# Attention over 16 heads: some copies of the turned keys moved to VectorE, waits moved to single products, and the next rows' two measures put side by side

## What is computed

```python
qkv = x @ Wqkv.T                                  # x: layernorm(x), b=8, t=512, D=256, 16 heads of 16
q = cos * q + rotate_half(q) * sin
k = cos * k + rotate_half(k) * sin
scores = jnp.einsum('bhqd,bhkd->bhqk', q, k) / math.sqrt(DH)
scores = jnp.where(causal, scores, -jnp.inf)
attn = jax.nn.softmax(scores, axis=-1)
out = jnp.einsum('bhqk,bhkd->bhqd', attn, v)
out = out.transpose(0, 2, 1, 3).reshape(b, t, d) @ Wo.T      # added to x
```

## Time and profile before

| | |
|---|---|
| median of 3 runs | 2533.52 us (2532.68 to 2536.14) |
| the profiled execution, its own time | 2531.52 us |
| its span in the trace | 2529.8 us |
| TensorE busy, share of the span | 2267.8 us, 90% |
| TensorE weight loads | 1748.3 us, 69% |
| VectorE | 1555.9 us, 62% |
| ScalarE | 1315.7 us, 52% |
| GpSimd | 922.6 us, 36% |
| second attention, 604 to 1204 us of the span: TensorE, VectorE, ScalarE, GpSimd busy | 481.69, 373.44, 339.30, 221.12 us |

### The profile page before, as it was taken

How to read it: one execution, slowest core, us unless ns; L and a number is a source line. 1 busy time by engine, 2 the same in 40 slices (tenths; PEclk the granted TensorE clock), 3 DMA queues, 4 the chain that set the end, 5 groups by cost and what they waited for, 6 DMA issues and landing times.

```text
span 2529.8 us, 45343 instructions
## 1 busy us (share of the span) xinstructions
PE 2267.8 (90%) x15874; PEld 1748.3 (69%) x15874; DVE 1555.9 (62%) x4796; ACT 1315.7 (52%) x3214; POOL 922.6 (36%) x1363
## 2 busy tenths in 40 slices
PE   7999599996778788877699999999999999999998
PEld 5777499994445363544567777777777777777777
DVE  6665422224666757565667676777777667776675
ACT  2221133333555755465555675666755675656753
POOL 2221122213434433332543344333544445343451
PEclk9999699998787988878899999999999999999999
DMA  3222411112001010100200000000101000000000
GB/s 132 100 100 90 130 36 37 39 30 79 19 10 59 3 59 11 35 35 11 88 9 18 16 3 18 18 18 10 44 26 62 19 9 26 26 26 18 10 18 26
DMA packets 75937, 96.41 MB, mean 38 GB/s; under 512 B 6113, under 2 KB 69090, under 8 KB 75458
## 3 DMA queue, kind: packets, MB, share of 16 engines
q1 hardware_dynamic: 70786, 81.89, 9.7%
q0 software_dynamic: 3408, 9.31, 1.3%
q10 hardware_dynamic: 1520, 2.31, 0.3%
HBM read 62.69 MB, written 30.28 MB: 37 GB/s over the span
## 4 chain that ended last, share of the span: by engine, by line
PE 27%; DVE 9%; ACT 8%; issue 5%; POOL 3%; DMA 0%; SPq 0%; DVEq 0%; POOLq 0%; ACTq 0%
PE l_free L2194 4%; PE l_free L2196 4%; PE l_free L2195 3%; PE l_out L2309 3%; PE l_score L2269 2%; POOL l_probs L1684 2%; PE l_turned L2290 2%; DVE l_probsT L1779 2%; DVE l_work L1856 2%; PE l_turned L2194 1%; PE l_turned L2196 1%; PE l_turned L2195 1%; DVE l_u_low L1862 1%; ACT l_probs L2068 1%; PE l_turned L2243 1%
## 5 line engine op out<-in xcount | busy, mean ns | idle before, releaser
L1684 POOL TENSOR_SCALAR l_probs<-l_probs,l_rinv 128x256 f32<-128x256 f32 (+1 forms) x512 | 223.5, 456 | 227.6 <-DVE l_rinv L1839 227.5
L1114 DVE CUSTOM_DVE_ANT_0 c_raw<-cbank,c_later 128x256 f32<-128x256 f32 (+3 forms) x512 | 218.3, 487 | 73.3 <-PE cbank L1301 73.0
L2068 ACT ACTIVATE l_probs<-l_probs,l_nmax 128x256 f32<-128x256 f32 (+1 forms) x512 | 239.9, 473 | 26.5 <-DVE l_nmax L1834 26.4
L1217 ACT ACTIVATE c_cprobsT<-cbank 128x384 f32<-128x384 f32 (+1 forms) x384 | 180.9, 525 | 95.8 <-PE cbank L1327 95.7
L1834 DVE CUSTOM_DVE_ANT_0 l_probs<-l_score,mask,l_inv 128x256 f32<-128x256 f32 (+1 forms) x512 | 200.0, 447 | 28.8 <-PE l_score L2269 28.1
L2194 PE MATMUL l_free<-l_part,l_w_high 128*128 128x512 f32 x384 | 166.4, 433 | 9.6 <-DVE l_probsT L1779 6.6
L2194 PE MATMUL l_free<-l_wqkv_high,l_yT 128*128 128x512 f32 x384 | 159.0, 414 | 1.9 <-DVE l_part L1758 1.9
L1817 DVE COPY l_probsT<-l_turned 128x512 f32<-128x512 f32 (+1 forms) x128 | 79.9, 624 | 131.3 <-PE l_turned L2290 80.3
L1006 POOL TENSOR_SCALAR_AFFINE_SELECT c_cprobsT<-c_cprobsT 128x256 f32<-128x256 f32 x256 | 99.6, 413 | 154.3 <-ACT c_cprobsT L1217 152.2
L2196 PE MATMUL l_free<-l_part,l_w_low 128*128 128x512 f32 x384 | 153.0, 398 | 0.0
L2195 PE MATMUL l_free<-l_yT,l_w_high 128*128 128x512 f32 x384 | 152.8, 398 | 0.0
(11 more groups left out here) (282 smaller groups left out, 5932.1 us busy)
## 6 DMA issues: line engine op xcount, KB each, us to landing
w<-in_W1T SPq DMA_DIRECT2D x8, 1024.0 KB, 8.0
w<-in_W2T SPq DMA_DIRECT2D x8, 1024.0 KB, 11.8
ys_d<-m_y SPq DMA_DIRECT2D x39, 128.0 KB, 1.7
xn_d<-a_prods SPq DMA_DIRECT2D x8, 512.0 KB, 3.6
c_came<-x_d SPq DMA_DIRECT2D x8, 512.0 KB, 4.9
y_d<-c_raw SPq DMA_DIRECT2D x8, 512.0 KB, 3.7
early_rows<-y_d SPq DMA_DIRECT2D x8, 512.0 KB, 3.7
l_came<-y_d SPq DMA_DIRECT2D x8, 512.0 KB, 3.9
```

The source lines that it names most:

```text
L1114: last = dve.tensor_tensor_reduce(raw[:, CHUNKS - NS + s, h * 2 * P:h * 2 * P + wide], score_place("scores", u, s)[:, h * 2 * P:h * 2 * P ...
L1217: act.activation(probsT[s][:, c % 2, i, k0:k0 + w], turned_place(j, s)[:, 0:w], ACT.Exp).then_inc(probs_ready[s], 1)
L1684: pool.tensor_scalar(a, a, rinv[:, j, r, h:h + 1], 1.0, ALU.mult, ALU.mult).then_inc(normed, 1)
L2068: act.activation(a, a, ACT.Exp, bias=nmax[:, j, r, h:h + 1], scale=-1.0, accum_out=rsum[:, j % 2, r, h:h + 1])\
```

## The change

Six things, all in `phase_attn1`:
- **Keys by VectorE.** For the last three turns of a pair (5, 6, 7) the two halves of the turned keys are copied to kT by VectorE (`keys_out`), after its last `parts`; ScalarE copies only their q. The copies count a semaphore of their own, `late_kT`, and TensorE waits for the one or the other count.
- **Order of the next pair's norm.** For every pair but the first, both rows are measured before the first is scaled.
- **Scores.** Each stream's wait for a free score bank stands at its own first product.
- **Turned scores.** Each stream's wait for exponentials stands at its own first product.
- **Output of the last chunk, part 0,** is made one step later, after piece 46 of the turned scores instead of before it.
- **The waits at unit 0** for all of qT, kT and v stand in a loop of their own.

```diff
--- before.py
+++ after.py
@@ -860,7 +860,7 @@
         qk_psum, v_psum, v_ready = sem2("cqk_psum"), sem2("cv_psum"), sem2("cv_ready")
         turned, rotated, high_ready = sem2("turned"), sem2("rotated"), sem2("high_ready")
         q_split, k_split = sem2("q_split"), sem2("k_split")
-        qkT_psum, qkT_ready = sem2("qkT_psum"), sem2("qkT_ready")
+        qkT_psum, qkT_ready, late_kT = sem2("qkT_psum"), sem2("qkT_ready"), sem2("late_kT")
         scores_ready, nmax_ready, probs_ready = sem2("cscores"), sem2("cnmax_r"), sem2("cprobs_r")
         nmax_high, nmax_split, nmaxT_psum, nmaxT_ready = sem("nmax_high"), sem("nmax_split"), sem("nmaxT_psum"), sem("nmaxT_ready")
         nmax_rows = [sem2(f"nmax_rows{i}") for i in range(2)]
@@ -872,6 +872,14 @@
         turns = [(s, t) for t in range(NT) for s in range(NS)]
         LAG = 3
+        late_keys = turns[-LAG:]
+
+        def copied(s, t, i):
+
+            late = sum(1 for r in range(t + 1) for k in (2, 3) if (s, r) in late_keys and (r, k) <= (t, i))
+            return 4 * t + i + 1 - late, late
+
+        ALL_COPIED = [copied(s, NT - 1, 3) for s in range(NS)]
@@ -1062,8 +1070,12 @@
                         whole_rows(0)
                         row_measure(0)
                         whole_rows(1)
-                        row_norm(0)
-                        row_measure(1)
+                        if trip:
+                            row_measure(1)
+                            row_norm(0)
+                        else:
+                            row_norm(0)
+                            row_measure(1)
                         row_norm(1)
                     def measure(s, done=0):
@@ -1100,6 +1112,12 @@
                         k = cosed[s][:, D:QK].rearrange("p (h d) -> p h d", d=DH1)
                         dve.wait_ge(high_ready[s], pair * (2 * NT) + 2 * (t + 1))
                         dve.tensor_tensor(khl[s][:, :, 3, :], k, khl[s][:, :, 0, :].bitcast(F32), ALU.subtract).then_inc(k_split[s], 1)
+
+                    def keys_out(s, t):
+                        for i in range(2):
+                            dve.wait_ge(qkT_psum[s], pair * (4 * NT) + 4 * t + 3 + i)
+                            dve.tensor_copy(kT[s][:, 4 * i:4 * i + 4, t * P:(t + 1) * P],
+                                            bank[s][2 + i][:].rearrange("p (a b) -> p a b", b=P)).then_inc(late_kT[s], 1)
                     def row_max(s, u):
                         c, qt, i, n = units[u]
@@ -1132,6 +1150,8 @@
                             turn(*turns[i])
                         if i:
                             parts(*turns[i - 1])
+                    for turned_late in late_keys:
+                        keys_out(*turned_late)
                     for u in range(UNITS):
                         for s in range(NS):
                             row_max(s, u)
@@ -1191,7 +1211,7 @@
                     for i in range(len(turns) + LAG):
                         if i >= LAG:
-                            for j in range(4):
+                            for j in range(2 if turns[i - LAG] in late_keys else 4):
                                 qkT_out(*turns[i - LAG], j)
                         if i < len(turns):
                             s, t = turns[i]
@@ -1268,7 +1288,10 @@
                         pe.wait_ge((q_split, k_split)[which][s], pair * NT + t + 1)
                         for i in (2 * which, 2 * which + 1):
                             if 4 * t + i >= 2:
-                                pe.wait_ge(qkT_ready[s], pair * (4 * NT) + 4 * t + i - 1)
+                                by_act, late = copied(s, *divmod(4 * t + i - 2, 4))
+                                pe.wait_ge(qkT_ready[s], pair * ALL_COPIED[s][0] + by_act)
+                                if late:
+                                    pe.wait_ge(late_kT[s], pair * ALL_COPIED[s][1] + late)
                             out = bank[s][2 + i % 2]
                             for a in range(4):
                                 p = 4 * (i % 2) + a
@@ -1288,14 +1311,16 @@
                     def scores(u):
                         c, qt, i0, n = units[u]
-                        for s in range(NS):
-                            if u == 0:
-                                pe.wait_ge(qkT_ready[s], pair * (4 * NT) + 4 * NT)
+                        if u == 0:
+                            for s in range(NS):
+                                pe.wait_ge(qkT_ready[s], (pair + 1) * ALL_COPIED[s][0])
+                                pe.wait_ge(late_kT[s], (pair + 1) * ALL_COPIED[s][1])
                                 pe.wait_ge(v_ready[s], pair * NT + NT)
-                            free_place("scores", u, s)
                         wide = max(2, qt + 1) * P
                         for i in range(n):
                             for s in range(NS):
+                                if i == 0:
+                                    free_place("scores", u, s)
                                 h = head(s, c, i0 + i)
                                 r, p = slice(64 * (h % 2), 64 * (h % 2) + 64), h // 2
                                 last = pe.matmul(score_place("scores", u, s)[:, i * 2 * P:i * 2 * P + wide], qT[s][r, p, qt * P:(qt + 1) * P],
@@ -1312,16 +1337,16 @@
                     def scores_turned(j):
                         c, i, kts = pieces[j]
-                        for s in range(NS):
-                            if j % PER_CHUNK == 0:
+                        if j % PER_CHUNK == 0:
+                            for s in range(NS):
                                 pe.wait_ge(nmax_rows[c % 2][s], pair * (16 * CHUNKS) + 32 * (c // 2 + 1))
-                            m = NS * j + s - 3
-                            if m >= 0:
-                                pe.wait_ge(probs_ready[m % NS], pair * UNITS + m // NS + 1)
                         for kt in kts:
                             q0 = min(kt, NT - 2)
                             at = 2 * P if kt == NT - 1 else 0
                             for s in range(NS):
+                                m = NS * j + s - 3
+                                if kt == kts[0] and m >= 0:
+                                    pe.wait_ge(probs_ready[m % NS], pair * UNITS + m // NS + 1)
                                 h = head(s, c, i)
                                 r, p = slice(64 * (h % 2), 64 * (h % 2) + 64), h // 2
                                 last = pe.matmul(turned_place(j, s)[:, at - (kt - q0) * P:at + (NT - kt) * P], kT[s][r, p, kt * P:(kt + 1) * P],
@@ -1365,7 +1390,11 @@
                         if 0 <= j < UNITS:
                             scores_turned(j)
                         for part in range(3):
-                            if j >= 3 and (j - 3 - 2 * part) % PER_CHUNK == 0 and 0 <= j - 3 - 2 * part < UNITS:
+                            if part == 0 and u == UNITS + SCORE_LAG - 3:
+                                continue
+                            if part == 0 and u == UNITS + SCORE_LAG - 2:
+                                output(CHUNKS - 1, part)
+                            elif j >= 3 and (j - 3 - 2 * part) % PER_CHUNK == 0 and 0 <= j - 3 - 2 * part < UNITS:
                                 output((j - 3 - 2 * part) // PER_CHUNK, part)
                     pe.wait_ge(raw_ready, pair * CHUNKS + CHUNKS)
                     for k in range(2 * NT):
```

## The result

Before: 2533.93 us (2532.68 to 2536.14, 4 runs). After: **2498.40 us** (2497.42 to 2499.67, 4 runs). The ratio is 0.9856 with a 95% interval of 0.9841 to 0.9872, a gain of 35.5 us. I forecast 15.4 us and a range down to 2509 us, so the prediction was wrong: the sign was right, the size less than half. The profiled execution took 2499.67 us.

What follows compares the result with a forecast made beforehand. No engine is full; only waits on the ring of engines count. The terms 1.8 + 6.0 + 2.2 + 1.6 + 3.8 = 15.4 us, taken from 2533.52, gave 2518.1 us (chance 0.63), range 2509 to 2526 us.

Steps and rivals of the forecast that it cites:

- Waits at single products: Turned scores: early stream 0 products save TensorE 2.2 us in whole chunks and 1.6 us in first chunks; bounds nothing and 8.4.
- The tail: End of each pair: piece 46 ahead of part 0 starts piece 47 0.95 us earlier, 3.8 us in four pairs.
- Order of the norm: Tails of pairs 0 to 2: TensorE's waits behind POOL ahead of part 0 go, 6.0 us; bounds nothing and 6.0.
- Part 0 itself: Tail: part 0 of the last chunk's output, now ahead of piece 47, is late next, then the last ban again.
- Bans beside scalings: Tail: POOL's bans beside VectorE's scalings slow by 0.1 us, covered; by the skill's port rule the sum would be 1.1 less.
- Keys: End of the projections: VectorE copying late keys brings the first scores 0.45 us earlier a pair, 1.8 us in four.
- Scores' waits: Scores: loosening stream 0's wait gives nothing, at most 0.3 us a pair, as VectorE works without a gap.
- middle chunks: Sign in the changed profile: a middle chunk of 8.4 instead of 8.53 us; still 8.53 would be wrong.
- only POOL's wait goes: Rival: the small savings, 9.4 us, are taken by whatever ends next; 6 to 8 us less, 2526.5 us; chance 0.16.
- POOL's wait stays: Rival: bans or the power of row set 1 are late for another reason; 2524.1 us; chance 0.07.
- the clock drops in the middle: Rival: split waits for piece 1 lose the upper clock, 1.5 us a middle chunk, 2548 us if all 20; chance 0.04.
- the clock stays up in the tails: Rival: without idleness 2.4 GHz holds in pairs 0 to 2, 2.2 us each, 6.6 more, 2511.5 us; chance 0.10.

Runs made afterwards that it cites:

- turned_alone: The kernel before with only the waits of the turned scores moved to each stream's first product; gain 15.0 us, ratio 0.9936.
- three: The kernel before with the norm's new order, the turned scores' waits at single products and part 0 of the last chunk one step later; 2502.15 us, ratio 0.9889.
- turned_out: The kernel before with the turned scores' waits at single products and part 0 of the last chunk one step later; gain 21.3 us, ratio 0.9923.
- no_norm: The changed kernel with the old order of the next pair's norm; gain 18.9 us against the kernel before, ratio 0.9931.
- fill_begin1: The changed kernel with one extra unread 512-column product in each of a pair's first 11 steps; gain 17.0 us against the kernel before, ratio 0.9936.
- keys_alone: The kernel before with only the late keys copied by VectorE; gain 2.1 us, ratio 0.9994 (0.9984 to 1.0005).
- scores_alone: The kernel before with only the scores' waits at each stream's first product, plus the loop of waits at unit 0; gain 1.5 us, ratio 0.9994.

## Why the prediction was wrong

What bounds the kernel was read rightly: no engine is full, the waits on the ring are what counts, and all but 0.9 of the 31.9 us lie in the four score stages and the joins between them. The medians of the five parts alone sum to 8.9 + 15.0 + 1.5 + 7.9 + 2.1 = 35.4 us, beside a measured gain of 35.5. That is in part luck and doesn't show that the parts simply add: the changed kernel's second measurement gained 31.7, and by the stages of their profiles the five parts come to 13.1 us of the 31.9, and in each of them the clock falls or rises in other places. The steps that failed are sizes.

- **Waits at single products: 3.8 us forecast, 15.0 measured alone** (interval 12 to 21; 9.1 placed by the stages). This step failed most. Two errors are seen in the middle chunk. Piece 1 gave 0.17 us, not 0.11: "saves only the 0.11 us between the two starts" forgot what follows it. (The rows that I named for "not much more than one alone" show no product alone; the line at 829.65 does, 0.39 us against 0.51 for two.) And I took piece 5 at nothing, "ahead of the DMA of the maxima"; it gave 0.10. Together 0.25 us by five chunks by four pairs is 5.0 us, where I had 2.2. The first chunks gave about the rest of the 8.2 us of the middles, 0.8 a pair, where I had 0.4; some of that is the clock, whose rise came 3.6 and 3.0 us after the first output product in pairs 0 and 2 before, and 1.9 and 1.8 after. And the tail, where I counted no wait of this kind for itself, gave 2.6 us more in joins and last tail. My upper bound of 0.3 us for each of 28 waits, 8.4 us, is what the middles gave (8.2, or 6.5 in turned_alone); I had it in the text and chose less than half of it.
- **The tail: 3.8 forecast, 7.2 in the stages, 7.9 by the median.** Piece 46 ahead of part 0 gave 1.5 us in pairs 0 and 1 alone and 1.3 in pair 3, where I took 0.95: about the whole step of 1.46 us from piece 46 to 47, which I had as upper bound. In pairs 0 to 2 part of it is POOL's delay, hidden behind piece 46, which I had given to the norm alone. "Part 0 itself" was late next, as predicted, and moving it again brought piece 47 only 0.45 us forward and no shorter tail.
- **Order of the norm: 6.0 forecast, 7.3 and 8.9 measured alone.** The mechanism is as told: powers side by side at 862.40, bans at 864.42, no wait for POOL ahead of part 0. The sum of idle times was a fair price alone, and too low in company: 7.7 us (three against turned_out) or 16.6 (the changed kernel against no_norm), both from medians on two chips. The step took the arrival of TensorE at part 0 from the trace of before, and other parts move it: the wait came to 8.7 us with the single waits alone, and back to 6.0 with the step later beside them (no_norm). "Bounds: nothing and 6.0" failed even alone. Pair 0's tail became 4.2 us shorter with a wait of 2.73, because the clock, counted separately as a rival, stayed up with it: an idle time in a trace isn't the most that its removal can bring.
- **Bans beside scalings.** 0.41 us each, beside eight scalings of 0.36, against 0.385 and 0.345 apart from each other: hardly stretched. The Trainium skill ("SBUF — State Buffer", "SBUF: two separate sides") has the one engine fully blocked while VectorE is in a mode that takes two ports; here both worked from 864.42 to 865.23. Whether the scalings run in such a mode no run shows, so this doesn't test the rule; it shows that it was no price to add here. Keeping the row's value was right. The 729.7 us at which I said the output wants the bans is worked out nowhere in the prediction; the sum doesn't use it.
- **The clock.** I gave 0.10 to a gain of 2.2 us a pair. What was found is a third thing: the stretch at the lower level, which before covered part of both tail and outputs (0.70 and 0.78 granted), now covers one of them. From the tails, 19.8 and 18.4 us, one is worth 1.4 us, and from the joins without and with it, 29.6 and 31.1, it is 1.5; so I estimate some 4 us in three joins. It belonged in the sum, since it is the parts together that bring it (pair 3 of turned_out). The Trainium skill ("TensorE: Matmul & The Clock Gate", "HAM oscillation — how this bites in real kernels") has long idle gaps drop the clock. The tails agree only in part: without POOL's wait all four kept it in one execution of the changed kernel and two of four in the other. And idle gaps give no reason for the starts of the pairs, where TensorE was 95% busy and at the lower level (fill_begin1).
- **Keys: 1.8 forecast, 1.6 us on the way to the first scores alone,** 0.2 to 0.3 a pair in company, and nothing measurable in the time. VectorE's copies took 0.62 us (2.47 us for four), not 0.69. The term was right for its own stage; in keys_alone the middle of pair 0, where the clock rose late, took it back.
- **Scores' waits: nothing forecast, nothing measurable.** The reason "VectorE works without a gap" was wrong: in the list of waits it stood 73.0 us in all for scores before, and 41.6 after. So was "at most 0.3 a pair": the stretch up to the first turned product gained 0.4 to 0.7 us a pair in scores_alone, which later stages took back.

Waits of VectorE for scores in the second attention, before:

```profile
DVE c_raw L1114 <- PE cbank L1301: 73.0, 86, 5.5
```

And after:

```profile
DVE c_raw L1132 <- PE cbank L1326: 41.6, 49, 2.1
```

Keys (0.4 to 0.5 us a pair) and middle chunks (8.53 to 8.4) were named as signs; the first came at 0.3 in the changed kernel, the second at 8.28. The rivals: *only POOL's wait goes* fell with turned_out, which gains 21.3 us with POOL's wait in place; *POOL's wait stays* fell with the waits list; *the clock drops in the middle* didn't happen, part 0 takes 1.06 us in the middle chunks of both kernels; *the clock stays up in the tails* came in part, as told above. The range was too narrow because I held each term to the idle time of one engine in one place. The three terms that missed all missed in the same direction. I read that as the ring at work, where every engine's earlier end makes the next one's start earlier; no run tests this by itself.

## What to carry to other kernels

On a ring of engines without a full one, a wait placed ahead of two products when each needs only its own can be worth more than the gap between their starts, and less than the idleness that goes: in turned_alone TensorE waited 21.5 us less for exponentials (39.6, then 18.1) and the time fell by 9.1 to 15.0 us. Count it at every place where it occurs. The worth of removing one engine's delay depends on what the other edits do to the arrival of the one that waits, so ask for each pair of parts whether the one makes the other's wait longer or hides it. An instruction moved behind the piece that feeds the next engine gave back about the whole step here, until the moved work itself stood in the way.
